# Conditional transformer block on one core: when GpSimd's weight chunks begin, and the order of the setup

## What is computed

```python
def rmsnorm(x, w):
    return x * jax.lax.rsqrt(jnp.mean(x * x, axis=-1, keepdims=True) + EPS) * w
def film(x, cond, w, b):
    scale, shift = jnp.split(cond @ w + b, 2, axis=-1)
    return x * (1.0 + scale[:, None, :]) + shift[:, None, :]
...
h = film(rmsnorm(x, norm1_w), cond, film1_w, film1_b)
Q = h @ q_w + q_b
K = h @ k_w + k_b
V = h @ v_w + v_b
scores = jnp.einsum('bnd,bmd->bnm', Q, K) * D ** (-0.5)
out = jnp.einsum('bnm,bmd->bnd', jax.nn.softmax(scores, axis=-1), V)
x = x + (out @ proj_w + proj_b)
h = film(rmsnorm(x, norm2_w), cond, film2_w, film2_b)
return x + jax.nn.gelu(h @ mlp_w1 + mlp_b1, approximate=False) @ mlp_w2 + mlp_b2
```

## Time and profile before

| | us |
|---|---|
| median of 3 runs (1761.38 to 1764.82) | 1761.59 |
| profiled execution | 1762.29 |
| its span, first to last instruction | 1760.5 |
| TensorE busy | 1750.2 (99%) |
| VectorE busy | 1294.1 (74%) |
| ScalarE busy | 890.3 (51%) |
| GpSimd busy | 217.2 (12%) |
| setup, up to the first key row of group 0 | 52.1 |
| groups, up to the first MLP product | to 528.5 |

### The profile page before, as it was taken

How to read it: one execution, slowest core, us unless ns; L and a number is a source line. 1 busy time by engine, 2 the same in 40 slices (tenths; PEclk the granted TensorE clock), 3 DMA queues, 4 the chain that set the end, 5 groups by cost and what they waited for, 6 DMA issues and landing times.

```text
span 1760.5 us, 23195 instructions
## 1 busy us (share of the span) xinstructions
PE 1750.2 (99%) x8318; PEld 1466.7 (83%) x8318; DVE 1294.1 (74%) x1743; ACT 890.3 (51%) x1498; POOL 217.2 (12%) x202
## 2 busy tenths in 40 slices
PE   9999999999999999999999999999999999999999
PEld 7788888888888888888888888888888888888887
DVE  5989898565665787588578758858875885885477
ACT  6554545545454555455455445545544554653344
POOL 0578786000000000000000000000000000000000
PEclk9999999999999999999999999999999999999999
DMA  9477778633236678768867876776787677677776
GB/s 349 142 284 274 261 295 280 228 108 103 79 110 199 196 254 278 203 206 275 249 194 257 274 203 212 272 247 193 259 273 202 219 270 242 190 241 246 195 225 205
DMA packets 202322, 395.83 MB, mean 225 GB/s; under 512 B 24160, under 2 KB 28256, under 8 KB 200160
## 3 DMA queue, kind: packets, MB, share of 16 engines
q1 hardware_dynamic: 202208, 394.34, 69.5%
HBM read 331.25 MB, written 62.98 MB: 224 GB/s over the span
## 4 chain that ended last, share of the span: by engine, by line
PE 91%; DVE 5%; ACT 2%; DMA 1%; issue 1%; SPq 0%; POOL 0%; ACTq 0%
PE psum L690 35%; PE psum L710 23%; PE psum L718 11%; PE psum L590 11%; PE psum L660 3%; PE psum L618 2%; PE psum L619 2%; PE psum L623 2%; DVE h_lo L1097 2%; DVE key_bias L1109 1%; DMA x_tok<-x_dram 1%; ACT x_tok L827 0%; ACT probs L982 0%; DVE key_bias L1106 0%; DMA wp_sb<-wp_dram 0%
## 5 line engine op out<-in xcount | busy, mean ns | idle before, releaser
L690 PE MATMUL psum<-op_hi_P,ring 128*128 128x512 f32 x1792 | 551.8, 389 | 0.0
L710 PE MATMUL psum<-stage_hi,ring 128*128 128x512 f32 x1784 | 440.6, 389 | 0.0
L690 PEld LDWEIGHTS psum<-op_hi_P,ring 128*128 128x128 f32 x1792 | 336.1, 188 | 69.6
L710 PEld LDWEIGHTS psum<-stage_hi,ring 128*128 128x128 f32 x1784 | 334.8, 188 | 69.5
L922 ACT CAST stage_hi<-x 128x1024 fp32r<-128x1024 f32 x224 | 235.4, 1054 | 235.2 <-PE psum L710 223.1
L690 PE MATMUL psum<-op_lo_P,ring 128*128 128x512 f32 x896 | 348.6, 389 | 0.0
L1301 DVE TENSOR_TENSOR stage_lo<-x,stage_hi 128x1024 fp32r<-128x1024 f32 x224 | 273.3, 1223 | 72.5 <-ACT stage_hi L922 72.2
L906 ACT ACTIVATE x<-x,vecs 128x512 f32<-128x512 f32 x192 | 138.0, 723 | 283.9 <-DVE x L1288 283.9
L718 PE MATMUL psum<-stage_lo,ring 128*128 128x512 f32 x892 | 238.4, 389 | 0.0
L690 PEld LDWEIGHTS psum<-op_lo_P,ring 128*128 128x128 f32 x896 | 168.2, 188 | 35.0
L718 PEld LDWEIGHTS psum<-stage_lo,ring 128*128 128x128 f32 x892 | 167.4, 188 | 34.8
(11 more groups left out here) (162 smaller groups left out, 2297.2 us busy)
## 6 DMA issues: line engine op xcount, KB each, us to landing
ring<-wu_scratch SPq DMA_DIRECT2D x448, 256.0 KB, 3.0
ring<-wd_scratch SPq DMA_DIRECT2D x448, 256.0 KB, 2.9
x_tok<-x_dram SPq DMA_DIRECT2D x16, 1024.0 KB, 9.9
xT_in<-xT_dram SPq DMA_DIRECT2D x16, 1024.0 KB, 8.2
x2T_scratch<-xT_in SPq DMA_DIRECT2D x32, 512.0 KB, 3.6
hn<-x2T_scratch SPq DMA_DIRECT2D x32, 512.0 KB, 5.4
xres<-x2T_scratch SPq DMA_DIRECT2D x32, 512.0 KB, 4.8
out_dram<-xres SPq DMA_DIRECT2D x31, 512.0 KB, 4.4
```

The lines of the kernel that those rows point to most:

```text
L690: mm = pe.matmul(to, wt, b, start=q in FRESH and t == 0, stop=t == len(steps) - 1, skip_group_check=True)
L710: mm = pe.matmul(bank(q, dt), a[:, dt, part, :], stage_hi[r][:, e, :], start=q in FRESH and ss == 0 and e == 0 and part == 0, stop=False, ...
```

## The change

1. GpSimd: every chunk n now waits for `key_done` of group n+1 (4(n+2) counts); the wait of chunk 0 for `probs_scaled` goes.
2. The queue: x^T of group 0 and the store of its rstd are issued behind two pairs of wvT/wp blocks instead of ahead of them and behind one; the norm row is loaded ahead of the last pair.
3. TensorE: 11 warm-up matmuls instead of 15; blocks 0 and 1 of the first product run pass by pass (all hi*hi, then lo*hi, then hi*lo), each pass waiting for its own operand; `v_product(n, 0)` runs ahead of `key_row(n)` in every group.
4. VectorE: `scale_x(0)` between weight blocks 1 and 2; `vp_low` right behind `h_low`; the wpT bias columns in the setup instead of in group 0.
5. ScalarE: `vp_high` ahead of `sum_squares(1)`; `sum_squares(2)` behind all of group 0's g.

```diff
-WARM_UP = 15
+WARM_UP = 11
@@ queue
-            load_xT(0)
             for k in range(KD):
-                if k == 1:
+                if k == 2:
+                    load_xT(0)
                     norm1_to_row(0)
+                if k == KD - 1:
+                    load_norm1_row(0)
                 sp.dma_start(wvT_sb[:, k, :], wvT[tokens(k), :]).then_inc(vp_loaded[k], 16)
                 sp.dma_start(wp_sb[:, k, :], wp[tokens(k), :]).then_inc(vp_loaded[k], 16)
-            load_norm1_row(0)
@@ GpSimd
                     if n == 0:
                         pool.wait_ge(vp_full, KD)
-                        pool.wait_ge(probs_scaled, 1)
+                    pool.wait_ge(key_done, KD * (n + 2))
                     sum_weights(n)
@@ TensorE
+            def weight_passes(k, into, full, a_hi, a_lo, b_hi, b_lo):
+
+                pe.wait_ge(weights_hi, 2 * k + 2)
+                for t, (a, b, lows) in enumerate(((a_hi, b_hi, 0), (a_lo, b_hi, 1), (a_hi, b_lo, 2))):
+                    if lows > 0:
+                        pe.wait_ge(weights_lo, 2 * k + lows)
+                    for c in range(KD):
+                        mm = pe.matmul(into[c], a[:, k, tokens(c)], b[:, k, :], start=k == 0 and t == 0,
+                                       stop=k == KD - 1 and t == 2)
...
             for k in range(KD):
-                weight_product(0, k, gv, prod_full, wq_hi, wq_lo, wk_hi, wk_lo)
+                if k < 2:
+                    weight_passes(k, gv, prod_full, wq_hi, wq_lo, wk_hi, wk_lo)
+                else:
+                    weight_product(0, k, gv, prod_full, wq_hi, wq_lo, wk_hi, wk_lo)
...
+                v_product(n, 0)
                 key_row(n)
-                v_product(n, 0)
                 scores(n)
@@ ScalarE
-            sum_squares(1)
             for c in range(KD):
                 vp_high(c)
+            sum_squares(1)
             act.wait_ge(wk_bq_done, KD)
-            keep_g(0, 0)
-            keep_g(0, 1)
+            for j in range(KD - 1):
+                keep_g(0, j)
+            key_high(0)
+            keep_g(0, KD - 1)
             sum_squares(2)
-            keep_g(0, 2)
-            key_high(0)
-            keep_g(0, 3)
@@ VectorE
                 weights_low(1, k, wvT_sb, wv_hi, wv_lo, wp_sb, wp_hi, wp_lo)
-            scale_x(0)
+                if k == 1:
+                    scale_x(0)
...
                 h_low(0, k)
+            for c in range(KD):
+                vp_low(c)
             bias_column(wk_sb, bq_row, wk_bq, wk_loaded, wk_bq_done)
...
             key_terms(0)
-            for c in range(KD):
-                vp_low(c)
             key_low(0)
+            bias_column(wpT_sb, bv_row, attn_col, wpT_loaded, wp_bv_done)
+            dve.wait_ge(wp_bv_done, KD)
+            dve.tensor_tensor(attn_col[:], attn_col[:], col("bp"), ALU.add).then_inc(attn_col_done, 1)
...
-                if n == 0:
-                    bias_column(wpT_sb, bv_row, attn_col, wpT_loaded, wp_bv_done)
-                    dve.wait_ge(wp_bv_done, KD)
-                    dve.tensor_tensor(attn_col[:], attn_col[:], col("bp"), ALU.add).then_inc(attn_col_done, 1)
```

More of the change, by code:

```diff
@@ L606, in weight_product @@
                         mm.then_inc(full, 1)
+            def weight_passes(k, into, full, a_hi, a_lo, b_hi, b_lo):
[6 more added lines that the diff above has]
+                                       stop=k == KD - 1 and t == 2)
+                        if k == KD - 1 and t == 2:
+                            mm.then_inc(full, 1)
             def g_product(m, j):
```

## The result

The changed kernel takes 1756.36 us (median of 6 runs, 1755.41 to 1757.12), the kernel before 1762.36 in the same session (6 runs, 1760.89 to 1764.82). The ratio is 0.9967, 95% interval 0.9957 to 0.9977: faster by 6.0 us, 0.34%. The forecast was 8.7 us and 1752.9.

A forecast was written before the change was run, and what follows sets the result against it. TensorE, busy 99% of the span, was taken as the bound, so only its waits could be won: 2.0 (second product and h) + 2.5 (first group) + 4.2 (groups) = 8.7 us, giving 1752.9, range 1750.5 to 1757.2.

The forecast's parts named there:

- Warm-up and first product: Setup on TensorE: four warm-up matmuls fewer start film 0.9 us earlier, worth nothing because a later wait swallows it.
- Second product and h: Setup: norm row lands at 27.4, TensorE waits 1.1 us before block 2, first g product at 36.7, gaining 2.0 us.
- rival (b): Setup: the norm row is late, a load of 4.5 to 6.9 us; total 1754.5 to 1757; chance 0.15.
- First group: Group 0: the 2.34 us gap before the key row plus its restart goes, gaining 2.5 us.
- Groups 1 to 8: Attention groups: chunks held until key_done leave h_lo and key terms free, winning 4.2 of 4.6 us of stalls.
- The margin: Groups: h_hi casts finish at 28 to 29.5 us, next product starts at 29.9, fitting by 0.4 us at worst.
- rival (c): Groups: a loop through x_tok stretches to 64.0 us per two periods, making the kernel slower, 1768; chance 0.05.
- x_tok 12: Block 12's late load has 1.9 us of room; ScalarE waits 1 to 3 us, exponentials have 5 us before TensorE's product.
- (a): Groups: the collision is only moved, h_hi 0.5 us late each group, groups' term about 0; 1757; chance 0.18 with (d).
- (d): Groups: the wait does nothing, w_src lands behind its release and chunks drift back; 1757; chance 0.18 with (a).
- if scaling starts past 29: Setup: sign of a wrong forecast; VectorE's scaling was expected at 27.4.
- The other rule, of the exclusive lock: Shared port pair locked per instruction: by it scaling takes about 1.3 us longer and the 0.4 us margin is gone.

The follow-up runs named there:

- store_first: The changed kernel with the store of rstd of group 0 issued ahead of the load of x^T on SP; 1754.13 us, ratio 0.9955.
- pool_only: The kernel before with only GpSimd's wait changed (each chunk held until key_done of the next group), setup untouched; 1757.84 us, ratio 0.9976.
- three_key_first: The changed kernel, both rstd stores and x_tok 12's load issued earlier, v_product(0, 0) behind key_row(0) again; 1753.01 us, ratio 0.9952.
- xtok12_first: The changed kernel with the load of x_tok block 12 put ahead of the loads of hn and f2w on SP; 1755.82 us, ratio 0.9963.
- row1_wpT_back: The changed kernel, store of rstd 1 ahead of x_tok 2, wpT columns and bp addition back behind exp_bias of group 0; 1757.31 us, ratio 0.9973.
- three_warm15: The changed kernel, both rstd stores and x_tok 12's load issued earlier, with 15 warm-up matmuls instead of 11; 1752.49 us, ratio 0.9944.
- three_warm7: The changed kernel, both rstd stores and x_tok 12's load issued earlier, with 7 warm-up matmuls instead of 11; 1752.31 us, ratio 0.9942.
- setup_only: The changed kernel with GpSimd's wait put back as before (probs_scaled ahead of the first chunk only); 1760.20 us, ratio 0.9991.

## Why the prediction was right or wrong

The direction, the range (1750.5 to 1757.2) and the main term were right; the forecast was 2.7 us (by the balance of the profiles 2.3) too hopeful, in two steps that the prediction itself had named as doubtful. A third came out right for another reason than the one given.

- **Warm-up and first product**, 0.9 us earlier. Film started only 0.4 us earlier: three intervals of the first product ran at half pace, the case that the prediction had in its last sentence there. As it said, the wait behind swallowed it. What it missed is the sign at the other end: in the two executions in which the early start came off in full, the wait was 3.7 to 4.0 us and the clock fell, which cost 2.4 to 2.6.
- **Second product and h**, +2.0: this is the step that failed. "I take 3.0, near the least" for the norm row's load; it took 4.6, near the median of its kind. From there all followed as written: wait of 2.1 us instead of 1.1, g product at 38.32 instead of 36.7. The gain was 0.3, rival (b)'s case. store_first showed that the 8.2 us from rstd done (16.0) to the store's landing (24.2) were the larger item: the sum had the landing right (24.3), but took the store's place behind x^T as given; ahead of x^T it landed 3.4 us earlier.
- **First group**, +2.5: measured 2.7. That all the gap went is right, but the main cause was read wrongly. The prediction put it down to v_product's move and an earlier h, and said that ScalarE's reordering costs nothing; by the rows the larger part belongs to that reordering. Of the 2.34 us of idle, VectorE stood 1.47 before key_lo for key_hi, which stood behind the squares of x_tok 2. In pool_only, with the old order, x_tok 2 landed 1.2 us earlier, VectorE stood 0.35 and the gap was 1.21: both times the rest is 0.9, which is also what v_product's move is worth in three_key_first. No run moves these squares alone.
- **Groups 1 to 8**, +4.2 of 4.6: all of it, and pool_only shows that the wait alone does it. Modulation took 4.92 us over the chunk, not 7.75, scaling 5.12; the chunk became 3.0 us shorter. The margin was forecast as 0.4 us at worst. TensorE's was enough; the loop through exp_bias, which the prediction did not see (its rival (c) closed a loop through x_tok), has none by the rows above.
- **x_tok 12**: "ScalarE waits 1 to 3 us there. The exponentials behind it ... have room for that." ScalarE waited 6.0 us, and TensorE lost 1.2. The landing took 15.1 us where the earlier trace rows had 13.9 as the longest, and the last chunk ended later by the key terms' delay, which began in group 0. The later squares of block 1, costed at nothing, and the wpT columns, for which 2.3 us of room were counted, lie in that delay; how it divides between them was not separated.
- **Rivals.** (b) came true: the row took 4.6 us, and its term lost 1.7. (a), (c) and (d) did not: the eight periods are 29.88 each. Of what would show it wrong, "if scaling starts past 29" was missed by 0.1 us (28.94). That the sum came as near as it did is in part luck: 0.5 us more than forecast in the groups and 0.2 more in the first one made up for some of the loss in the setup.

The prediction cited the Trainium skill, "TensorE: Matmul & The Clock Gate", part 1, on the rise of the clock differing from run to run. The runs agree, see below. The other rule, of the exclusive lock, was given 1.3 us and a rival; the lock shows (see below), and no g product of groups 1 to 9 waited for it.

## What to carry to other kernels

When a wait puts one engine's batch behind another's, write down the loop that this closes and its length against the period of the bounding engine; if they are equal, whatever is late once can stay late, and come out far away, here nine groups on, where a queue adds its own delay. Follow a wait back through every engine that stands in it: the gap before the key row began with squares on ScalarE that waited for a load, and the row on TensorE names only VectorE's key_lo. A tiny transfer whose result is waited for (a 2 KB store) belongs ahead of the megabytes in the same queue. And an earlier start that only meets a longer wait is not neutral for TensorE: twice it went with a fall of the clock.

## What the runs showed of the hardware

- **The clock's rise.** The warm-up always starts at 1.53, with records 0.213 us apart, later 0.111. The change came at about 4.4 us in xtok12_first and row1_wpT_back, 5.4 in three_warm15, 6.4 in the kernel before, 7.7 in the changed kernel and 9.0 in three_warm7. "TensorE: Matmul & The Clock Gate", part 1, in the Trainium skill says that the point varies from run to run; the traces agree: with the same 11 warm-up matmuls it lay between 4.4 and 7.7 us.
- **The clock's fall.** Behind 4.0 us of idle (xtok12_first) and 3.7 (row1_wpT_back) the granted clock was 0.50 (1.2 GHz); behind the 2.1 of the changed kernel and the 2.4 of setup_only it stayed at 1.00. The falls cost 2.4 and 2.6 us.
- **The lock.** An addition of 128x4 numbers on VectorE, 0.16 us alone, took 1.29 in groups 1 to 8 of the changed kernel, while GpSimd's subtraction of 1.29 us ran. That is how the Trainium skill, "SBUF — State Buffer", section "Who interferes with whom", tells it: whoever comes second is blocked for the whole instruction. GpSimd's power (170.04, 1.34 us) again did not hold up VectorE: the scaling and modulations over it ran at 0.68 and 0.33 us, as when alone.
